# Moving dense-layer blocks into an attention's last steps, exponentials behind the next gate, and the experts' end two half-steps forward

## The reference, cut to what matters

```python
x = x + _L0_xattn_ref(_layernorm(x), ctx, Wq, Wk, Wv, Wo, gq, gk)   # 16 heads of 128, keys from ctx
x = x + _L0_ffn_ref(_layernorm(x), W1, b1, W2, b2, W3, b3)          # 512 -> 1024 -> 1024 -> 512, relu
x = x + _L1_xattn_ref(_layernorm(x), ctx, pos, pos, Wq, Wkv, Wout, bout)
x = x + _L1_ffn_ref(_layernorm(x), W_q, keys, down_embed, up_embed, gate_w, up_w, down_w)
```

## Time and profile before

| | us |
|---|---|
| median of 3 runs | 2046.19 |
| the runs | 2047.24, 2046.19, 2042.27 |
| the profiled execution | 2046.22 |
| its span, first to last instruction | 2044.4 |
| mean granted clock of PE | 0.991 |

### The profile page before, as it was taken

The page is one execution under the profiler, slowest core; times in us unless marked ns, Lnnn a source line. Parts: engine busy times, 40 slices in busy tenths (PEclk is TensorE's granted clock), DMA queues, the critical chain, the costliest instruction groups (busy, mean ns, idle before and its releaser), DMA issues. The chain is left out here.

```text
span 2044.4 us, 33384 instructions
## 1 busy us (share of the span) xinstructions
PE 1992.8 (97%) x12656; PEld 1646.3 (81%) x12656; DVE 1288.2 (63%) x2265; ACT 794.4 (39%) x2371; POOL 530.1 (26%) x579
## 2 busy tenths in 40 slices
PE   6999999999999999999999999999999999999998
PEld 5888888888888887878888777777787788888886
DVE  5555555665555555342435488888757877887787
ACT  5555555655555543211112355454432222122211
POOL 3222222321223324410103243332210222222231
PEclk9999999999999999999999899999999999999999
DMA  6100000200011112120104100000112355554555
GB/s 231 51 5 5 8 5 10 78 28 29 29 57 52 50 32 82 52 83 0 62 29 128 59 20 21 18 21 16 45 52 72 134 181 185 190 189 158 188 174 185
DMA packets 76487, 154.16 MB, mean 75 GB/s; under 512 B 8816, under 2 KB 31088, under 8 KB 76400
## 3 DMA queue, kind: packets, MB, share of 16 engines
q0 software_dynamic: 23712, 87.04, 12.8%
q1 hardware_dynamic: 52688, 65.97, 9.8%
HBM read 136.21 MB, written 16.78 MB: 75 GB/s over the span
## 5 line engine op out<-in xcount | busy, mean ns | idle before, releaser
L2351 POOL DMA_INDIRECT m_ring<-in_table,m_row x128 | 126.3, 987 | 391.2 <-DVE l_x_all L2464 284.8
L48 PE MATMUL four_banks<-l_yT_hi,m_hi 128*128 128x512 f32 x512 | 199.4, 390 | 0.0
L48 PE MATMUL four_banks<-l_yT_lo,m_hi 128*128 128x512 f32 x512 | 199.2, 389 | 0.0
L1121 DVE TENSOR_SCALAR f_relu<-bank,f_b 128x512 f32<-128x512 f32 x64 | 47.9, 749 | 165.1 <-ACT f_h_hi L1064 165.1
L511 ACT ACTIVATE prob<-four_banks,mx,rms 128x128 f32<-128x128 f32 x256 | 114.0, 463 | 92.1 <-DVE mx L645 92.1
L1064 ACT ACTIVATE f_h_hi<-bank,f_b 128x512 fp32r<-128x512 f32 x64 | 44.1, 689 | 262.9 <-PE bank L48 262.9
L289 POOL TENSOR_TENSOR rms<-ssq,constants 128x8 f32<-128x8 f32 x64 | 13.0, 204 | 435.9 <-ACT junk L496 263.8
L2328 ACT ACTIVATE m_act_of<-m_dot,l_ln_y 128x2 f32<-128x2 f32 x64 | 18.9, 296 | 241.4 <-DVE m_junk L2454 241.4
L48 PEld LDWEIGHTS four_banks<-l_yT_hi,m_hi 128*128 128x128 f32 x512 | 96.1, 188 | 20.2 <-issue 0.2
L48 PEld LDWEIGHTS four_banks<-l_yT_lo,m_hi 128*128 128x128 f32 x512 | 96.1, 188 | 19.8
L48 PE MATMUL four_banks<-wo_hi,oT_hi 128*128 128x512 f32 x256 | 106.4, 416 | 4.7 <-DVE oT_lo L660 4.7
(11 more groups left out here) (304 smaller groups left out, 5584.3 us busy)
## 6 DMA issues: line engine op xcount, KB each, us to landing
f_stage<-in_w POOLq DMA_DIRECT2D x14, 512.0 KB, 4.5
f_x_in<-x SPq DMA_DIRECT2D x18, 256.0 KB, 2.9
ctx_in<-in_ctxT SPq DMA_DIRECT2D x32, 128.0 KB, 2.5
x_in<-in_x SPq DMA_DIRECT2D x16, 256.0 KB, 2.6
x<-xres SPq DMA_DIRECT2D x16, 256.0 KB, 2.0
x<-l_x_all SPq DMA_DIRECT2D x16, 256.0 KB, 2.0
m_stage<-in_gate SPq DMA_DIRECT2D x8, 512.0 KB, 6.2
m_stage<-in_up SPq DMA_DIRECT2D x8, 512.0 KB, 7.3
```

The costliest lines, as they stand in the source:

```text
L48: mm = pe.matmul(out, st, mv, start=first and n == 0, stop=last and n == len(terms) - 1)
L1121: dve.tensor_scalar(relu[m % 2][:], bank[HB[m % 2]][:], b12[:, layer, m:m + 1], 0.0, ALU.add, ALU.max).then_inc(S["relu_ready"], 1)
L2351: pool.indirect_dma_start(ring[slot][:], None, table, bass.IndirectOffsetOnAxis(ap=row[:, tile_of(g), k:k + 1], axis=0)).then_inc(S[f"got{ ...
```

## The change

In the first attention the dense layers' transposes of tiles 0 and 1 move from step 31 to step 30, with their layer norms (to step 29), statistics and roots (to step 28) and loads (to step 27); those of tiles 2 and 3 stay in step 31, at other places. `hidden1` of blocks 0 and 1 moves into step 31, blocks 2, 3 and 4 are in step 32 (`BEGUN = 5`). The keys' two banks are swapped. Weight piece 4 is split, and piece 6 fetched, inside POOL's step 31, between the two `means`. In the last layer `exps(n)` is queued on ACT behind the next even half-step's `gates`. `LATEST` = 62: the 64 groups spread over half-steps 9 to 61, two groups in 9, 13, 18, 23, 28, 33, 37, 42, 47, 52 and 57, and the last `add_experts` in half-step 62. The diff, with one line of context ahead of each edit:

```diff
@@ -318,8 +318,6 @@
                 means(s, 1)
-            if now == STEPS - 1:
-                ahead["root"](pool, 0, 3)
@@ -358,7 +356,7 @@
             pairs = [((ctxp[0][:, k, :], ctxp[1][:, k, :]), (wkp[g][0][:, k, :], wkp[g][1][:, k, :])) for k in range(KC)]
-            product(pe, bank[(5, 4)[g]][:], pairs).then_inc(S[f"k_made{g}"], 1)
+            product(pe, bank[(4, 5)[g]][:], pairs).then_inc(S[f"k_made{g}"], 1)
@@ -423,37 +421,39 @@
                 turn_x(s + 1)
-            if now == STEPS - 1:
-                ahead["turn_x"](pe, 0, 0)
                 if now == STEPS:
-                    ahead["hidden1"](pe, 0, 0)
+                    ahead["hidden1"](pe, 0, 2)
             if now == STEPS:
-                ahead["hidden1"](pe, 0, 1)
+                ahead["hidden1"](pe, 0, 3)
                 mix(s - 1, 1)
-            if now == STEPS - 1:
-                ahead["turn_x"](pe, 0, 1)
                 queries(s, 1)
+                if now == STEPS - 1:
+                    ahead["turn_x"](pe, 0, 2)
             if now == STEPS:
-                ahead["hidden1"](pe, 0, 2)
+                ahead["hidden1"](pe, 0, 4)
                 score(s, 0)
+                if now == STEPS - 1:
+                    ahead["turn_x"](pe, 0, 3)
             if now == STEPS - 1:
-                ahead["turn_x"](pe, 0, 2)
+                ahead["hidden1"](pe, 0, 0)
                 queries(s + 1, 0)
+            if now == STEPS - 2:
+                ahead["turn_x"](pe, 0, 0)
@@ -464,10 +464,12 @@
                 turn_q(s + 1, 0)
+            if now == STEPS - 2:
+                ahead["turn_x"](pe, 0, 1)
             if now == STEPS - 1:
-                ahead["turn_x"](pe, 0, 3)
+                ahead["hidden1"](pe, 0, 1)
@@ -493,7 +495,7 @@
             for j in range(G):
-                a = act.activation(junk[g][:, G + j, :], bank[(5, 4)[g]][:, j * D:(j + 1) * D], ACT.Square,
+                a = act.activation(junk[g][:, G + j, :], bank[(4, 5)[g]][:, j * D:(j + 1) * D], ACT.Square,
@@ -525,10 +527,9 @@
                 exps(s - 1, 1)
-            if now == STEPS - 1:
-                ahead["split_x_hi"](act, 0, 0)
             if now == STEPS:
-                ahead["hidden_hi"](act, 0, 0, 0)
+                for m in range(1, 4):
+                    ahead["hidden_hi"](act, 0, 0, m)
@@ -540,12 +541,10 @@
                 split_o(s - 1, 1)
-            if now == STEPS:
-                ahead["hidden_hi"](act, 0, 0, 1)
             if now == STEPS - 1:
-                ahead["split_x_hi"](act, 0, 1)
+                ahead["split_x_hi"](act, 0, 2)
@@ -564,16 +563,18 @@
                 split_hi(act, "wo0", now // NB)
+            if now == STEPS - 1:
+                ahead["split_x_hi"](act, 0, 3)
                 exps(s, 0)
-            if now == STEPS - 1:
-                ahead["split_x_hi"](act, 0, 2)
                 copy_v(s, 1)
+                if now == STEPS - 2:
+                    ahead["split_x_hi"](act, 0, 0)
@@ -581,8 +582,10 @@
                 square_q(s + 1, 0)
+            if now == STEPS - 2:
+                ahead["split_x_hi"](act, 0, 1)
             if now == STEPS - 1:
-                ahead["split_x_hi"](act, 0, 3)
+                ahead["hidden_hi"](act, 0, 0, 0)
@@ -630,7 +633,7 @@
             dve.tensor_tensor(k_sb[g][:].rearrange("p (h d) -> p h d", h=G),
-                              bank[(5, 4)[g]][:].rearrange("p (h d) -> p h d", h=G),
+                              bank[(4, 5)[g]][:].rearrange("p (h d) -> p h d", h=G),
@@ -681,40 +684,47 @@
                 split_o(s - 1, 0)
+            if now == STEPS:
+                ahead["hidden_lo"](dve, 0, 0, 0)
                 normalise(s - 1, 1)
+                if now == STEPS:
+                    ahead["hidden_lo"](dve, 0, 0, 1)
                 copy_pT(s - 1, 1)
-            if now == STEPS - 3:
+            if now == STEPS - 4:
                 ahead["statistics"](dve, 0, 1)
-            if now == STEPS - 2:
+            if now == STEPS - 3:
             if now == STEPS - 1:
-                ahead["split_x_lo"](dve, 0, 0)
+                ahead["split_x_lo"](dve, 0, 1)
+                ahead["statistics"](dve, 0, 2)
             if now == STEPS:
-                ahead["hidden_lo"](dve, 0, 0, 0)
+                ahead["hidden_lo"](dve, 0, 0, 2)
             if now == STEPS - 1:
-                ahead["statistics"](dve, 0, 2)
+                ahead["layer_norm"](dve, 0, 2)
+                ahead["statistics"](dve, 0, 3)
             if now == STEPS:
-                ahead["hidden_lo"](dve, 0, 0, 1)
+                ahead["hidden_lo"](dve, 0, 0, 3)
+                ahead["hidden_lo"](dve, 0, 0, 4)
             if now == STEPS - 1:
-                ahead["split_x_lo"](dve, 0, 1)
-                ahead["layer_norm"](dve, 0, 2)
+                ahead["split_x_lo"](dve, 0, 2)
+                ahead["layer_norm"](dve, 0, 3)
@@ -729,7 +739,7 @@
             if now == STEPS - 1:
-                ahead["statistics"](dve, 0, 3)
+                ahead["split_x_lo"](dve, 0, 3)
@@ -738,11 +748,10 @@
                 normalise(s, 0)
-            if now == STEPS - 1:
-                ahead["split_x_lo"](dve, 0, 2)
-                ahead["layer_norm"](dve, 0, 3)
                 copy_q(s + 1, 0)
+            if now == STEPS - 2:
+                ahead["split_x_lo"](dve, 0, 0)
@@ -751,8 +760,6 @@
                 split_lo(dve, "wo1", 0)
-            if now == STEPS - 1:
-                ahead["split_x_lo"](dve, 0, 3)
@@ -768,7 +775,7 @@
     HB = (4, 5)
-    BEGUN = 3
+    BEGUN = 5
@@ -876,14 +883,16 @@
             fetch(sp, 1)
-        if s == AHEAD_FROM + 4:
-            sp.wait_ge(A["stored"], 16 * 12)
+        if s == AHEAD_FROM + 3:
+            sp.wait_ge(A["stored"], 16 * 11)
             load_x(sp, 0, 1)
+        if s == AHEAD_FROM + 4:
             sp.dma_start(b12[:, 1, :], b2).then_inc(S["b12_loaded"], 16)
+        if s == 2 * NB - 2:
+            load_x(sp, 0, 2)
         if s == 2 * NB - 1:
-            load_x(sp, 0, 2)
@@ -942,12 +951,15 @@
             fetch(pool, i + 2)
-        if s == 2 * NB - 3:
+        if s == 2 * NB - 4:
             root(pool, 0, 2)
+            root(pool, 0, 3)
+            split_lo(pool, 4)
+            fetch(pool, 6)
@@ -964,7 +976,7 @@
-        for i in range(4, len(ORDER)):
+        for i in range(5, len(ORDER)):
@@ -1069,7 +1081,7 @@
         def step(c, first=False, last=False):
-            for m in range(2 if first else 0, KH):
+            for m in range(4 if first else 0, KH):
@@ -1132,7 +1144,7 @@
             chain[0] = 0
-            for m in range(2 if first else 0, KH):
+            for m in range(5 if first else 0, KH):
@@ -2121,7 +2133,7 @@
-    FIRST = 2 * ROUTES + 1
+    FIRST, LATEST = 2 * ROUTES + 1, 2 * STEPS - 2
@@ -2197,7 +2209,7 @@
     for g in range(GROUPS):
-        taken[FIRST + g * (2 * STEPS - FIRST) // GROUPS].append(g)
+        taken[FIRST + g * (LATEST - FIRST) // GROUPS].append(g)
@@ -2332,8 +2344,8 @@
                     gates(act, n, j)
-                if j == 1 and n < ROUTES:
-                    exps(n)
+                if j == 0 and 0 < n <= ROUTES:
+                    exps(n - 1)
@@ -2493,7 +2505,8 @@
                     pending.append(g)
-        add_experts(pending.pop())
+                if 2 * n + j == LATEST:
+                    add_experts(pending.pop())
```

## The result

The changed kernel took **2022.86 us** (median of 6 runs, 2021.73 to 2026.05) against 2043.98 (6 runs, 2041.45 to 2047.24) of the kernel before in the same job: ratio 0.9903, 95% interval 0.9892 to 0.9914. It is faster, by about 1%. The profiled execution took 2025.97 us, with a span of 2024.2, so the span fell by 20.2 us where the sum said 18.6.

What follows compares the result with a forecast made beforehand. PE bounds the kernel, busy 1992.8 of 2044.4 us, so only its gaps and low clock can be won. 12.4 + 3.1 + 3.1 = 18.6 us off 2046.2 gave 2027.6 us, range 2023.5 to 2035.5.

Steps and rivals of the forecast that it cites:

- Part A: First attention's last steps: 13.3 us of PE gaps and low clock, less 0.9 us of new waits, gives 12.4 us.
- Where the low clock comes: First attention's end: low clock only beside gaps summing to 3.3 and 4.7 us, so none expected with gaps up to 0.4.
- three places with gaps worth a change: First attention's end (7.97 us), the last layer's start (1.62, 1.44, 1.20 us), and the tail (DVE works on 4 us).
- The split on POOL: Step 31: `split_lo(4)` starts 0.4 us after DVE's layer norm of tile 3; whichever starts first locks the shared ports.
- Rival 1: Step 31: POOL's split starts first, DVE's layer norm waits 1.9 us, a low stretch costs 2.6; 2032 us, chance 0.14.
- Part B: Last layer's start: gate ahead of exponentials saves DVE 2.2 us three times; PE gains 3.1 us, bounds 3.06 and 0.
- both gaps, 1.62 + 1.44 = 3.06 us, vanish: Last layer's start: with DVE only about 2.6 and 2.0 us late, two PE gaps go, priced at idle time.
- The doubles, net 0: Last layer's two-group half-steps: the 1.20 us gap goes, about 1.1 comes back behind 13 and 37; within 1.2 either way.
- Part C: Tail: experts end two half-steps sooner, so `add_y` follows PE tile by tile; gain 3.1 us, bounds 3.2 and 0.
- Rival 4: Tail: the experts' earlier end gains nothing, because the stores set the end; 2030.7 us, chance 0.06.
- Rival 3: Step 31: tile 3's load comes late and holds `hidden1(0, 0)`; slower than before, 2053 us at 30 us late, chance 0.02.
- The four cases called faster: Forecast 0.65, Rival 1 0.14, gathers stalling PE at doubles 0.10, Rival 4 0.06; their sum was given as 0.94.

Runs made afterwards that it cites:

- no_lock_before: Kernel before, only ACT's cuts of weight blocks 4 and 5, and POOL's low parts with them, moved to the end of step 32: 2038.35 us, ratio 0.9971.
- a_only: Changed kernel with both last-layer edits (exponentials and experts) undone, leaving only the attention part: 2031.62 us, ratio 0.9935 to the kernel before.
- split_first: Changed kernel with ACT's cut of weight block 4 ahead of the copy of tile 2's transpose: 2024.79 us, ratio 0.9901 to the kernel before.
- doubles_odd: Changed kernel with its eleven two-group half-steps all at odd places, in close pairs: 2029.08 us, ratio 0.9926 to the kernel before.
- order_before: no_lock_before with ACT's copy and DVE's low part of the last x tile put behind `split_o(31, 0)`: 2035.81 us, ratio 0.9964 to the kernel before.
- no_fill: Changed kernel with `hidden1`'s five products put back where the kernel before has them: 2028.13 us, ratio 0.9915 to the kernel before.
- c_only: Kernel before with only the `LATEST` spread of the groups and the earlier last `add_experts`: 2043.79 us, ratio 0.9993.
- b_only: Kernel before with only the exponentials queued behind the next gate: 2041.50 us, ratio 0.9985.

## Why the prediction was right, point by point

- **Part A, 12.4 us**: 12.65 by the marks. The walk through the queues held in its order and nearly in its sizes: 0.4 us was said for `turn_p(31, 0)` and 0.34 measured; the 0.2 at `output(30, 0)` did not come, and of the 0.2 at `hidden1(0, 0)` 0.1 did. What the working did not say is how the gain divides. It was told as filling holes with matmuls; the runs show that half (6.8 us of 13.4 by the medians of no_lock_before and a_only) to two thirds (8.3 of 12.65 by the marks) is had by taking POOL's weight splits away from DVE's operations, and that the moved matmuls bring 2.4 to 3 us on top.
- **Where the low clock comes.** The working said that it came only beside gaps that summed to 3.3 and 4.7 us, and took from this that small gaps bring none. The second half held (the clock is 1.00 in the windows above), the first was a misreading: the same profile has the low level at two places more. Windows of the kernel before, the first row behind gaps of 1.91 and 1.43 us at the start of the second attention, the second behind gaps of 1.07, 0.95 and 0.84 us near its end:

```profile
1159.00:1170.00 11.00, 9.57 (x84) 7.70 (x76) 2.35 (x6) 5.22 (x5) 5.24 (x3) 0.53 0.01 1
```

```profile
1476.00:1482.00 6.00, 5.83 (x44) 4.68 (x48) 3.08 (x4) 3.42 (x4) 0.12 (x1) 0.72 0.00 0
```

  The prediction also named three places with gaps worth a change. The start of the second attention is a fourth: PE stands still there for 0.79 + 0.50 + 1.91 + 1.43 = 4.63 us (4.65 in the changed kernel), more than part B took away, and with the low clock beside it.
- **The split on POOL**: the working said that whoever starts first decides, by 0.4 us. In the changed kernel it was 0.38 us, in DVE's favour, and split_first turned it round with the result that DVE was held. The Trainium skill's rule (SBUF — State Buffer, "SBUF: two separate sides", an exclusive lock for the whole instruction) agrees with the 2.44, 2.03, 1.44 and 1.25 us rows: each such DVE operation ended 0.02 to 0.55 us behind POOL's split, never before it. (The prediction had "ended only when POOL did"; the 128x512 ones still had some of their own work left then.) Rival 1's price was too high by a factor of more than ten.
- **Part B, 3.1 us**: 3.6 in the changed kernel, by the shift of PE's products over half-steps 6 and 8. The term that was mis-sized is "both gaps, 1.62 + 1.44 = 3.06 us, vanish": a gap costs more than its recorded idle time. Behind the gap of 1.20 us the chain of the kernel before has a block of twelve at 3.05 us, where it takes 2.72:

```profile
1703.90 3.05 PE bank L48 x12
```

  DVE's lateness at the two places was forecast as 2.6 and 2.0 and came to 2.54 and 2.04. The wait of 2.21 us that went was not table load and Silu alone, as the prediction had it: ACT's exp took 0.23 us, the table load 1.28, and Silu 0.60 directly behind it. ACT stands idle for no more than 0.02 us on either side of the load, so the about 4 us that the prediction had for a switch with a drain do not apply here. Timeline of ACT in the kernel before:

```profile
1565.18 0.23 ACT L2323 ACTIVATE m_ex<-m_best 128x32 f32<-128x32 f32 x1 [6.10 <-DVE m_best L2427]
1565.43 1.28 ACT L2304 ACT_TABLE_LOAD   x1
1566.72 0.60 ACT L2304 ACTIVATE m_gated<-four_banks 128x512 f32<-128x512 f32 x1
```

- **The doubles, net 0**: net 0.9 us gained between the two profiles. The gap at 22 took 1.5 us with it (1.20 and the slower block), against 0.66 lost at 38. Part of that is luck of the profile that was priced, since the gap at 22 was nil in another execution of the same last layer. Behind the double at 13 the forecast lateness of 4.8 to 6.0 was 3.8; behind 18 it was 4.6 (said 4.7), behind 28 3.9 (3.9), behind 37 5.8 (5.6 to 6.8).
- **Part C, 3.1 us**: 3.3. `add_y` ran at PE's pace. Rival 4 (the stores set the end) is out.
- **Rival 3**, the late load of tile 3: nothing waited for it.
- **The range** was too narrow below. Its low end had 4.1 us for everything: 0.9 of waits in A, 1.2 at the doubles and 2 for the runs. The terms came out 1.6 us better in sum, and the starting point, 2046.2 as the median of three runs, came down to 2044.0 with the six that were measured; that is 2.2 of the 4.7 us by which the median missed the forecast. (The four cases called faster sum to 0.95, not 0.94.) Runs that lie 5 us apart should have had more than 2 us.

## What to carry to other kernels

When PE stands still behind a DVE operation that takes three times its usual time, look at what POOL runs in that moment: moving two of POOL's splits gained more here than the matmuls that then filled the holes. Price a gap of PE at its idle time plus about 0.3 us, and count how late the feeding engine is at each step, since a change that takes lateness off early (B) also pays for one that adds it later (C). Do not price a single gap from a single profile when a gather stands behind it: the one at half-step 22 was 1.20 us in one execution and nil in another. Spread extra work evenly when its data come through a ring: eleven doubles in close pairs cost about 5 us more than the same eleven spread out.

## What the runs showed of the hardware that was not expected

- **Restart after a gap.** A block of twelve matmuls behind a gap took 3.05 us in the chain, else 2.72, at a clock of 1.00. From its first start to the start of the next block it is 2.89 us (1703.90 to 1706.79), so 0.17 us is slower matmuls; the other 0.16 is the overlap of a matmul with the next (0.39 us long, 0.23 from start to start), which is lost when none follows. PE's products were shifted by 1.88 and 1.70 us at gaps recorded as 1.62 and 1.44, and in doubles_odd by 1.89 at one of 1.73.
- **POOL and DVE beside each other, in the dense layers.** POOL can be held too: six of its splits in the kernel before, each begun 0.14 to 0.15 us behind a 128x512 operation of DVE that reads two tensors, neither of them a bank, took 2.79 to 2.81 us; the others took 2.33 to 2.40. And the start of the split alone does not decide. In the changed kernel one such operation of DVE began 0.29 us ahead of a split and still ended 0.55 us behind it, 3.25 us long; POOL was issuing a DMA when it began. That the DMA's issue held it is a reading of these rows (three more profiles of kernels with this part have the same), not an experiment:

```profile
802.71 0.94 POOL L851 DMA_DIRECT2D f_stage<-in_w  x1 [0.30 <-POOL f_w_lo L864]
...
803.38 3.25 DVE L1136 TENSOR_TENSOR f_h_lo<-f_relu,f_h_hi 128x512 fp32r<-128x512 f32 x1
...
803.67 2.41 POOL L864 TENSOR_TENSOR f_w_lo<-f_stage,f_w_hi 128x1024 fp32r<-128x1024 f32 x1
```

- **The low clock is not a function of the gaps alone.** no_lock_before and order_before have the same three gaps (0.72, 0.83 or 0.84, 0.48 or 0.47) in the same places; the one kept 1.00, the other had 3.4 us at the lower level. no_fill kept it with gaps of 1.55 and 1.41. c_only, which is the kernel before up to there, had 3.4 and 6.8 us of it where the kernel before and b_only had 6.8 and 6.8. What else decides was not found.
- **Scatter of the runs.** The marked product of attention lay between 668.9 and 673.9 us in thirteen profiles of kernels that are alike up to there but for the two swapped banks and two moved loads; the earliest had no low clock in the start-up, the latest 6.8 us of it.
